# Softmax sums inverted on VectorE instead of ScalarE, VectorE operations over two PSUM banks, and new instruction orders in a three-part transformer block

## The chip, the cores and the metric

One core of one Trainium2 chip runs the whole program as one launch. The metric is the device time of an execution in microseconds (us); the time of a kernel is the median of its timed runs. The engines of the core that matter here are TensorE (PE in the rows; PEld is its loading of weights), VectorE (DVE), ScalarE (ACT), GpSimd (POOL) and SyncE (SP), which issues the DMAs.

## The reference

Input `x` is 4 x 1024 x 256 in float32. Three parts follow each other, each on a layer-normalised input and added to the residual:

```python
x = x + _L0_attn_ref(_layernorm(x), ...)              # 16 heads of 16: a gated delta rule with short convolutions
x = x + _L0_xattn_ref(_layernorm(x), ctx, ctx, ...)   # differential cross-attention on 64 context rows
x = x + _L0_ffn_ref(_layernorm(x), ...)               # depthwise conv, top 2 of 8 experts, a small GELU network

def _sdpa(q, k, v):                                    # in _L0_xattn_ref, 2 x 16 heads of 8
    scores = jnp.einsum('bhqd,bhkd->bhqk', q * SCALE, k)
    p = jax.nn.softmax(scores, axis=-1)
    return jnp.einsum('bhqk,bhkd->bhqd', p, v)
a1, a2 = _sdpa(q1, k1, v), _sdpa(q2, k2, v)
attn = a1 - lam * a2                                   # then a norm over 16 and a projection
```

The change touches the softmax of the cross-attention (its maxima, its sums) and, in the first part, small steps of the convolution and of the delta rule.

## The kernel before

The 1024 positions are worked in 8 blocks of 128, for all 4 batches at once (512 columns). Each block's work is cut into a `first` half (the delta rule) and a `second` half (cross-attention and the expert network). Work is pipelined over blocks: in pass i (the loop of `turns`, line 642) run the second half of block i-1, and three parts of the first halves of blocks i, i+1 and i+2. The passes run from -2 to 8. Passes -2 and -1 follow the order "start", pass 0 "head", passes 1 to 6 "steady", pass 7 "drain", pass 8 "last".

Inside a pass, nothing decides the order at run time: the table `ORDERS` lists for every engine and stage the names of its steps, one after the other. A step without a prefix belongs to the first half of block i, `+` to that of i+1, `*` to that of i+2, `-` to the second half of block i-1. Every engine works off its list in order, and waits at a step for semaphores that other engines raise (`up`, `fin`). An instruction that waits holds all that follow it on its engine. `KEEP` adds filler matmuls (line 1811) ahead of certain TensorE steps of the stages other than "steady".

The cross-attention of a block is worked in 8 units u, two per batch. Of a unit:

- `sc` (TensorE, line 2103): scores into two PSUM banks, half a = 0 and half a = 1, 512 columns (8 heads by 64 context rows) each. In the steady order these are banks 4 and 5, in the last pass banks 0 and 1 take turns with them.
- `max` (VectorE, lines 1582 and 1588): step 0 takes the maximum of each head, one reduction for each bank; step 1 subtracts it, one instruction for each bank. Each half's subtraction raises the semaphore `psub`, for which the next unit's scores into that bank wait.
- `max` (ScalarE, line 1037): the exponential of 1024 columns.
- `pt` (TensorE and ScalarE, lines 2125 and 1045): transposes in two halves, each copied out of PSUM.
- `pv` (TensorE, line 2139): the products with the values and with ones, so that the sums of the softmax stand in PSUM beside the numerators.
- `den` (ScalarE, lines 1053 and 1054): the reciprocal of the sums as exp(-ln(s)), 128x256: a logarithm out of PSUM into SBUF, then the exponential in place.
- `av` (VectorE, lines 1598 and 1601): numerator times reciprocal (semaphore `a_num`, for which the next unit's transposes into the same bank wait), and a1 - lam a2.

Steps of the first half that the change touches, all on VectorE: `conv` (lines 1353 and 1364 copy the three columns of halo in and out of `pre`, one block of 128 channels at a time, six each per pass), `dsel` and `gsub` (lines 1402, 1408, 1418: the decay matrix out of PSUM banks 2 and 3, one instruction for each bank), `zc` (line 1482: two instructions of 256 columns out of banks 2 and 3, eight times per pass). `solve` is a chain of small steps that inverts 16 x 16 triangles, `s`, `m` and `o` (lines 1499, 1492, 1510 and 1513) carry the state from chunk to chunk; they share VectorE with the attention in a pass.

The attention part of VectorE's steady order reads, in part:

```
-max.0.0 -max.0.1 -max.1.0 am.0 -max.1.1 am.1 -av.0.0 am.2 +cond -av.0.1 -max.2.0 -max.2.1 am.3 -av.1.0 solve.0.0
... -max.6.0 -max.6.1 zc.1 -av.4.1 -av.5.0 s.0 -max.7.0 zc.2 m.1 -max.7.1 -av.5.1 zc.3 -av.6.0
```

## Time and profile before

| what | value |
|---|---|
| median of 3 runs | 1374.06 us (1372.43 to 1379.7) |
| profiled execution | 1380.29 us, its span 1378.5 us |
| mean granted TensorE clock | 0.989 of full speed |
| busy, share of the span: TensorE / VectorE / ScalarE / GpSimd | 94% / 83% / 66% / 15% |
| instructions: TensorE / VectorE / ScalarE | 17045 / 3060 / 1760 |
| a pass of the steady order (mean of 6) | 155.4 us |

All times of rows are of the profiled execution and count from its span's start. Busy time is the union of an engine's instructions; an engine that waits for a semaphore is idle. On VectorE consecutive instructions overlap a little: the next begins before the one ahead of it has ended, so that durations add up to more than the time they hold the engine.

### The profile page before, as it was taken

The numbers are of one execution on the slowest core, as the hardware profiler recorded it, in microseconds if no ns is written. First come the engines' busy times: TensorE is split into PE (matmuls) and PEld (weight loads), VectorE is DVE, ScalarE is ACT, GpSimd is POOL, SyncE is SP. The second block draws the span as 40 slices with busy tenths as digits, with TensorE's granted clock in tenths as the row PEclk, the third lists the DMA queues.
The fourth block names the chain that finished last, engine by engine and source line by source line (L and its number), as shares of the span: only waits on it lengthen the run. The fifth ranks groups of instructions, "written<-read, shape, count | busy, mean of one in ns | idle before, by whom it ended". The sixth has DMA issues, their size and how long they took to land.

```text
span 1378.5 us, 40816 instructions
## 1 busy us (share of the span) xinstructions
PE 1291.2 (94%) x17045; PEld 838.7 (61%) x17077; DVE 1139.6 (83%) x3060; ACT 907.6 (66%) x1760; POOL 206.8 (15%) x204
## 2 busy tenths in 40 slices
PE   6988899899999999899999999999999989899998
PEld 5665666646765566646765566646765567646754
DVE  6567899988898989988898989988898878966763
ACT  2564477756877577756877577856877466644664
POOL 1031111102301122102301122102301112101000
PEclk9999999999999999999999999999999999999999
DMA  7021020101110020101100010101100001000000
GB/s 271 8 48 32 3 45 4 33 2 32 32 33 2 2 58 6 34 1 30 35 33 2 2 55 10 34 1 32 32 18 3 1 32 17 19 1 16 2 1 16
DMA packets 22782, 35.77 MB, mean 26 GB/s; under 512 B 1992, under 2 KB 18504, under 8 KB 22344
## 3 DMA queue, kind: packets, MB, share of 16 engines
q1 hardware_dynamic: 22600, 33.17, 8.6%
q8 instruction: 136, 2.23, 0.7%
q14 instruction: 46, 0.38, 0.1%
HBM read 20.56 MB, written 8.39 MB: 21 GB/s over the span
## 4 chain that ended last, share of the span: by engine, by line
PE 68%; DVE 16%; ACT 10%; issue 4%; DMA 1%; POOL 0%; SPq 0%; DVEq 0%; ACTq 0%
PE bank L2210 14%; PE four L1970 5%; PE bank L1884 5%; PE bank L1757 4%; PE bank L1782 4%; PE bank L2125 4%; PE bank L2103 3%; PE bank L2139 3%; PE four L1989 2%; PE four L1782 2%; PE bank L1886 2%; ACT L833 2%; PE bank L1811 2%; PE four L2014 2%; PE bank L1789 2%
## 5 line engine op out<-in xcount | busy, mean ns | idle before, releaser
L2210 PE MATMUL bank<-w_sb,cs 128*128 128x512 f32 x512 | 248.7, 602 | 2.9 <-ACT qkv L1109 0.4
L798 POOL TENSOR_TENSOR decayed<-state,pk 128x512 f32<-128x512 f32 x64 | 76.1, 1189 | 671.3 <-DVE state L1499 671.3
L2210 PEld LDWEIGHTS bank<-w_sb,cs 128*128 128x128 f32 x512 | 92.4, 189 | 95.8 <-issue 71.5
L1109 ACT ACTIVATE cs<-bank 128x512 f32<-128x512 f32 x112 | 66.9, 598 | 99.2 <-PE bank L1763 48.8
L833 ACT ACT_TABLE_LOAD x82 | 105.2, 1283 | 1.5
L1357 DVE SCALAR_TENSOR_TENSOR qkv<-pre,l_sb,qkv 128x512 f32<-128x512 f32 x144 | 101.6, 751 | 0.0
L1884 PE MATMUL bank<-hT,w_sb 128*128 128x512 f32 x192 | 95.2, 619 | 3.9 <-ACT hid L913 2.2
L1696 DVE SCALAR_TENSOR_TENSOR cs<-cs,rwt 128x256 f32<-128x256 f32 x196 | 88.2, 485 | 6.2 <-ACT cs L1109 2.8
L1045 ACT COPY cs<-bank 128x512 f32<-128x512 f32 x114 | 66.0, 579 | 41.3 <-PE bank L2125 41.2
L1582 DVE TENSOR_REDUCE pkc<-bank 128x8 f32<-128x512 f32 x116 | 74.3, 682 | 21.1 <-PE bank L2103 20.0
L1811 PEld LDWEIGHTS bank<-c_sb 128*128 128x128 f32 x588 | 74.6, 199 | 11.3 <-issue 10.3
L1811 PE MATMUL bank<-c_sb 128*128 128x128 f32 x588 | 81.1, 287 | 0.0
L1499 DVE SCALAR_TENSOR_TENSOR state<-four,c_sb,decayed 128x128 f32<-128x128 f32 x256 | 71.5, 341 | 9.5 <-PE four L2014 9.5
L1037 ACT ACTIVATE cs<-cs 128x1024 f32<-128x1024 f32 x60 | 63.2, 1053 | 24.2 <-DVE cs L1588 24.0
L2125 PE MATMUL bank<-c_sb,cs 128*128 128x128 f32 x456 | 72.6, 282 | 5.6 <-ACT cs L1045 2.4
L1970 PE MATMUL four<-kq,shared 64*64 64x48 f32 x2048 | 71.2, 224 | 5.5 <-POOL shared L780 4.6
L2014 PEld LDWEIGHTS four<-rq,shared 32*64 32x64 f32 x2048 | 45.7, 133 | 50.0 <-issue 31.9
L2014 PE MATMUL four<-rq,shared 32*64 32x64 f32 x2048 | 63.6, 231 | 13.4 <-issue 4.3
L1588 DVE TENSOR_TENSOR cs<-bank,pkc 128x512 f32<-128x512 f32 x116 | 74.2, 681 | 0.9
L1970 PEld LDWEIGHTS four<-kq,shared 64*64 64x64 f32 x2048 | 66.7, 140 | 13.3 <-issue 13.1
L1513 DVE SCALAR_TENSOR_TENSOR M<-four,c_sb,M 128x128 f32<-128x128 f32 x192 | 66.7, 347 | 4.0
L2020 PE MATMUL four<-shared,rq 32*64 32x64 f32 x2048 | 63.5, 232 | 4.8 <-issue 2.2
(297 smaller groups left out, 2990.9 us busy)
## 6 DMA issues: line engine op xcount, KB each, us to landing
xt<-in_x SPq DMA_DIRECT2D x8, 512.0 KB, 4.8
vscr<-qkv SPq DMA_DIRECT2D x8, 512.0 KB, 2.6
vT<-vscr SPq DMA_DIRECT2D x32, 128.0 KB, 4.5
Tm<-in_x SPq DMA_DIRECT2D x8, 512.0 KB, 3.8
out<-cs SPq DMA_DIRECT2D x8, 512.0 KB, 2.9
w_sb<-in_weights SPq DMA_DIRECT2D x1, 3680.0 KB, 19.1
rotb<-swapped SPq DMA_DIRECT2D x16, 128.0 KB, 2.3
swapped<-rota SPq DMA_DIRECT2D x16, 128.0 KB, 2.3
```

The source lines that it names most:

```text
L798: fin("dec", tt(decayed[:, :, :, :], state[:, :, :, :], eGC[:, c, :].unsqueeze(1).unsqueeze(3).to_broadcast([P, 4, G * B, DH]), ALU.mult))
L833: nc.scalar.preload_act_table_set(name)
L1357: ins = stt(dst, pre[:, n % 4, :, t:TB + t], L("conv", 4 * n + t, 4 * n + t + 1), dst, ALU.mult, ALU.add)
L1582: highest[a] = link(red(mx[:, a, :], sc[a], AX.X, ALU.max))
L1696: ins = stt(comb[:, b, :], src, wgt, comb[:, b, :], ALU.mult, ALU.add)
L1782: last = mm(dst[:, D * n:D * n + D], lhs[:, k, b * TB:b * TB + TB], rhs[:, k, :], start=False, stop=n == 1 and k == 1)
L1811: mm(bank[7 if i > 0 else 6][:, 0:P], ident, ident, start=True, stop=True)
L1884: mm(dst, ctrl[:, k, at:at + P], hT[:, k, :], start=k == 0, stop=False)
L1970: last = mm(bank[RAW[c % 4]][q, 48 * n:48 * n + 48], kqb[q, c % 2, n, :], kq[q, g, b, c, :, :].rearrange("p x t -> p (x t)"), start=True, ...
L2014: return mm(dst, zc_ring[p_, c % 4, 2 * a + g, 1, :], rq[p_, c % 2, (2 * a + g) * 64:(2 * a + g) * 64 + 64].rearrange("p (h v) -> p h v", ...
L2125: last = nc.tensor.transpose(turned_bank(j, u, n)[:, h * P:h * P + P], prob[:, 4 * n + h, :], ident)
L2210: mm(dst, x1T[:, k, b * TB:b * TB + TB], ew[:, k, ep * 512:ep * 512 + 512], start=k == 0, stop=False)
```

## The change

ScalarE's step `den` goes, with its two instructions per unit, and VectorE gets a step `den` with one reciprocal per unit, straight out of PSUM. Banks 4 and 5 become one tensor of two banks, as banks 0 to 3 are already, so that one VectorE instruction can span both. `max`, `dsel`, `gsub` and `zc` then take one instruction where they took two, and `conv` copies the halo of two channel blocks at once. For `zc` the constant `zx` is stored twice as wide. `psub` is raised once a unit instead of twice, so the scores of the next unit wait for the whole subtraction, and the first reduction waits for both halves of the scores. All five stages have new orders on all four engines, and `KEEP` has other counts.

```diff
         four = ctx.enter_context(nc.psum_tensor("four", [P, 4, 512], F32))
-        bank = [four[:, n, :] for n in range(4)] + [ctx.enter_context(nc.psum_tensor(f"bank{n}", [P, 512], F32)) for n in range(4, 8)]
+        four45 = ctx.enter_context(nc.psum_tensor("four45", [P, 2, 512], F32))
+        bank = [four[:, n, :] for n in range(4)] + [four45[:, n, :] for n in range(2)] + [ctx.enter_context(nc.psum_tensor(f"bank{n}", [P, 512], F32)) for n in range(6, 8)]
...
+        def both_scores(j, u):
+
+            return four[:, 0:2, :] if j == NI - 1 and (u % 2 or u >= 4) else four45[:, :, :]
...
-                def den_(u):
-                    log_exp()
-                    up("pv_ps", u + 1)
-                    if u:
-                        up("a_num", u)
-                    o_s = values_bank(j)[:, :].rearrange("p (f x t) -> p f x t", f=2, x=2)
-                    ch.do(A(den, o_s[:, :, 1, :], ACT.Ln))
-                    fin("den", A(den, den, ACT.Exp, scale=-1.0))
...
-                        for a, n in enumerate(pair):
-                            tap[a] = ch1.link(V.tensor_copy(pre[:, n % 4, :, 0:3], halo[:, n, :, :]))
+                        at = 2 * m % 4
+                        tap[0] = tap[1] = ch1.link(V.tensor_copy(pre[:, at:at + 2, :, 0:3], halo[:, 2 * m:2 * m + 2, :, :]))
...
-                        for a, n in enumerate(pair):
-                            fin("halo", V.tensor_copy(halo[:, n, :, :], pre[:, n % 4, :, TB:TB + 3]))
+                        at = 2 * m % 4
+                        fin("halo", V.tensor_copy(halo[:, 2 * m:2 * m + 2, :, :], pre[:, at:at + 2, :, TB:TB + 3]))
...
-                        for n in range(2):
-                            masked[n] = link(tt(M3[:, 32 * n:32 * n + 32, :], bank[2 + n][:, :].rearrange("p (n t) -> p n t", t=CH),
-                                                C("eye16").unsqueeze(1).to_broadcast([P, 32, CH]), ALU.mult))
+                        masked[0] = link(tt(M3[:, 0:NP_, :], four[:, 2:4, :].rearrange("p a (n t) -> p (a n) t", t=CH),
+                                            C("eye16").unsqueeze(1).to_broadcast([P, NP_, CH]), ALU.mult))
...
-                    zx = C("zx").unsqueeze(1).to_broadcast([P, G, P])
-                    for a in range(2):
-                        last = stt(zc_ring[:, c % 4, 2 * a:2 * a + 2, :, :].rearrange("p n x m -> p n (x m)"), bank[2 + a][:, 0:D].rearrange("p (n m) -> p n m", m=P), C("x0"), zx, ALU.mult, ALU.add)
-                    fin("zc", last)
+                    ring = flat(zc_ring[:, c % 4, :, :, :].rearrange("p n x m -> p n (x m)")).rearrange("p (a n) -> p a n", a=2)
+                    fin("zc", stt(ring, four[:, 2:4, 0:D], C("x0"), C("zx").unsqueeze(1).to_broadcast([P, 2, D]), ALU.mult, ALU.add))
...
                 def max_(u, k):
-                    sc = [scores(j, u, a)[:, :].rearrange("p (h n) -> p h n", h=8) for a in range(2)]
+                    sc = both_scores(j, u).rearrange("p a (h n) -> p (a h) n", h=8)
                     depth = 2 if j == NI - 1 else 1
-                    if k == 0 and j == NI - 1 and u:
-                        up("psub", 2 * u)
                     if k == 0:
-                        for a in range(2):
-                            up("sc_ps", 2 * u + a + 1)
-                            highest[a] = link(red(mx[:, a, :], sc[a], AX.X, ALU.max))
+                        if j == NI - 1 and u:
+                            up("psub", u)
+                        up("sc_ps", 2 * u + 2)
+                        highest[0] = link(red(flat(mx), sc, AX.X, ALU.max))
                         return
                     if u >= depth:
                         up("pt_ps", 2 * (u - depth) + 2)
-                    for a in range(2):
-                        ch.wait(highest[a])
-                        fin("psub", tt(prob_of(j, u)[:, 512 * a:512 * a + 512].rearrange("p (h n) -> p h n", h=8), sc[a], bc(mx[:, a, :], NK), ALU.subtract))
+                    ch.wait(highest[0])
+                    fin("psub", tt(prob_of(j, u).rearrange("p (h n) -> p h n", h=16), sc, bc(flat(mx), NK), ALU.subtract))
+
+                def den_(u):
+                    up("pv_ps", u + 1)
+                    o_s = values_bank(j)[:, :].rearrange("p (f x t) -> p f x t", f=2, x=2)
+                    fin("den", V.reciprocal(den, o_s[:, :, 1, :]))
...
-                    up("psub", 2 * (u - depth) + 1 + a) if u >= depth else up("qx_sb")
+                    up("psub", u - depth + 1) if u >= depth else up("qx_sb")
```

The same part of VectorE's steady order after the change:

```
-max.0.0 -max.0.1 am.0 -max.1.0 +cond -max.1.1 -den.0 -av.0.0 -av.0.1 am.1 am.2 -max.2.0 -max.2.1 am.3 -den.1 solve.0.0
... -max.6.0 -av.4.1 -max.6.1 zc.1 -den.5 -av.5.0 s.0 -max.7.0 zc.2 m.1 -max.7.1 -av.5.1 zc.3 -den.6
```

In the steady order `-max.u.1` stands right behind `-max.u.0` for u = 0 and u = 2. Summed over their entries, the fillers of `KEEP` are 119 in pass -1, 64 in pass 0, 63 in pass 7 and 44 in pass 8 before, and 109, 69, 54 and 44 after; pass -2 has 4 in both.

## Rows read from the trace of the kernel before

**Rows 1.** The page's first lines: busy us, share, instructions; then the chain's shares by engine.

```profile
PE 1291.2 (94%) x17045; PEld 838.7 (61%) x17077; DVE 1139.6 (83%) x3060; ACT 907.6 (66%) x1760; POOL 206.8 (15%) x204
...
PE 68%; DVE 16%; ACT 10%; issue 4%; DMA 1%; POOL 0%; SPq 0%; DVEq 0%; ACTq 0%
```

**Rows 2.** Stretches: length, busy us (instructions) of PE, PEld, DVE, ACT, POOL; granted clock, DMA, GB/s.

```profile
76.40:189.12 112.72, 97.18 (x1586) 67.71 (x1585) 89.55 (x234) 59.43 (x117) 22.41 (x22) 0.91 0.11 28
...
499.81:655.85 156.04, 148.97 (x2054) 94.28 (x2059) 138.82 (x372) 111.97 (x218) 25.31 (x24) 1.00 0.09 22
...
965.81:1121.55 155.74, 147.93 (x2038) 93.47 (x2043) 130.29 (x348) 107.35 (x212) 25.35 (x24) 0.98 0.06 16
1121.55:1269.40 147.85, 138.64 (x2073) 95.81 (x2079) 116.54 (x313) 86.96 (x178) 21.38 (x22) 1.00 0.05 13
1269.40:1378.50 109.10, 99.41 (x716) 65.43 (x717) 62.57 (x171) 61.03 (x113) 2.54 (x2) 1.00 0.03 11
```

**Rows 3.** Stretches of one steady pass, and the fullest 20 us of the neighbouring one.

```profile
499.81:579.81 80.00, 75.42 (x1262) 51.99 (x1266) 72.72 (x179) 63.39 (x132) 15.22 (x16) 1.00 0.12 29
579.81:655.85 76.04, 73.55 (x811) 42.30 (x797) 66.10 (x194) 48.58 (x87) 10.09 (x8) 1.00 0.06 15
...
404.93:424.93 20.00, 18.10 (x430) 11.41 (x416) 19.58 (x53) 17.15 (x37) 4.01 (x3) 1.00 0.02 4
```

**Rows 4.** VectorE's waits in one steady pass: who waited for whom, us, times, longest.

```profile
DVE cs L1598 <- ACT cs L1054: 2.6, 2, 1.8
DVE pkc L1582 <- PE bank L2103: 2.1, 1, 2.1
```

**Rows 5.** Groups by form: ScalarE's two steps, then VectorE's product: busy, mean ns, idle.

```profile
L1053 ACT ACTIVATE cs<-bank 128x256 f32<-128x256 f32 x56 | 21.0, 374 | 21.5 <-PE bank L2139 21.5
L1054 ACT ACTIVATE cs<-cs 128x256 f32<-128x256 f32 x64 | 26.7, 417 | 2.0
...
L1598 DVE TENSOR_TENSOR cs<-bank,cs 128x256 f32<-128x256 f32 x56 | 23.3, 417 | 16.7 <-ACT cs L1054 15.7
```

**Rows 6.** The chain through one unit: start us, us, what.

```profile
557.17 0.38 ACT cs L1053
...
558.02 0.44 DVE cs L1598
```

**Rows 7.** Reciprocals by form, a product of as few elements, then min/median/max of the reciprocals.

```profile
L1670 DVE RECIPROCAL rwt<-rwt 128x4 f32<-128x4 f32 x7 | 1.3, 180 | 0.2
...
L1671 DVE TENSOR_TENSOR rwt<-rwt 128x4 f32<-128x4 f32 x7 | 1.2, 167 | 0.2
...
L1670 DVE RECIPROCAL rwt<-rwt 128x2 f32<-128x2 f32 x2 | 0.3, 168 | 0.1
...
L1670 DVE RECIPROCAL rwt<-rwt x9: 167/180/183, 290.1 to 1338.2; 128x4 f32<-128x4 f32 x7, 128x2 f32<-128x2 f32 x2
```

**Rows 8.** VectorE's instructions in order of time, two places: start us, us, what.

```profile
509.09 1.22 DVE L1423 SCALAR_TENSOR_TENSOR M<-M,c_sb 128x1024 f32<-128x1024 f32 x1
510.23 1.29 DVE L1393 SCALAR_TENSOR_TENSOR kq<-kn,hid 128x512 f32<-128x512 f32 x2
...
538.71 1.28 DVE L1582 TENSOR_REDUCE pkc<-bank 128x8 f32<-128x512 f32 x2
539.91 1.28 DVE L1588 TENSOR_TENSOR cs<-bank,pkc 128x512 f32<-128x512 f32 x2
...
551.39 1.41 DVE L1357 SCALAR_TENSOR_TENSOR qkv<-pre,l_sb,qkv 128x512 f32<-128x512 f32 x2
552.72 0.87 DVE L1482 SCALAR_TENSOR_TENSOR shared<-four,c_sb 128x256 f32<-128x256 f32 x2
553.50 1.28 DVE L1582 TENSOR_REDUCE pkc<-bank 128x8 f32<-128x512 f32 x2
```

**Rows 9.** Stretches of passes 7 and 8 that hold the attention.

```profile
1121.55:1201.55 80.00, 74.74 (x1368) 58.40 (x1368) 71.70 (x178) 55.07 (x117) 14.62 (x17) 1.00 0.09 22
1280.00:1320.00 40.00, 38.76 (x449) 28.89 (x448) 30.02 (x64) 27.64 (x51) 0.00 (x0) 1.00 0.01 2
```

More of the change, by code:

```diff
@@ new lines @@
+        d1.0 -pw.1.0 -pw.0.1 -moe.6 wo.2 -pt.9 -pv.3 -turn5.1 -moe.5 -ffd.1 cs.4.1 *turn1.1 *rot -moe.9 cs.7.1 -moe.19
+        -sc.2.1 -sc.4.1 -turn4.1 d1.4 -moe.31 -wp.0.1 -pv.5 -sc.5.1 -moe.14 -pt.15 cs.6.1 cs.3.0 onorm.1 -pt.3 -moe.10
+        -pt.10 +sum.0 +sum.1 cs.4.0 -moe.29 -moe.25 cs.0.0 -qx.0.0 *gate.0 co.1 -sc.0.0 -moe.12 -pt.5 co.0 wo.1 z.3
+        -pt.4 -moe.16'''),
+        "dve": steps('''
+        solve.0.0 solve.11.0 am.1 -max.2.0 -acc.0.0 -dconv.1.0 zc.3 m.3 o.5.1 am.2 -av.6.1 -max.3.0 -max.0.0 +cond
@@ new lines @@
+        -sc.6.1 -pv.1 -moe.17 -ffu.1 cs.6.0 cs.6.1 -moe.18 -pv.0 -pv.5 -sc.7.0 *turn1.0 d1.7 -sc.5.1 *turn1.1 cs.7.0
+        -moe.21 -moe.31 cs.7.1 -moe.11 -moe.29 -moe.20 *rot co.0 -mo.0.0 -moe.0 co.1 -moe.3 onorm.0 -ffd.0 wo.0 -pt.11
+        -pv.3 onorm.1 -moe.25 -rturn.1 *gate.0 +sum.0 -pt.5 -qx.1.1 -ffd.1 -sc.7.1 wo.1 -mo.1.0 -pw.0.1 wo.2 +sum.1'''),
+        "dve": steps('''
+        -den.1 -av.7.1 norm.0 -av.6.1 -max.2.0 norm.1 dsel.0 -den.3 dsel.1 gsub.0 norm.2.0 -max.7.1 -hnorm.1 norm.3.0
@@ new lines @@
+        cs.7.0 cs.7.1 -turn6.1 *rot -router.0 co.0 co.1 -ffd.0 -ffd.1 onorm.0 -ffu.0 -ffu.1 onorm.1 *gate.0 wo.0
+        +sum.0 wo.1 wo.2 +sum.1'''),
+        "dve": steps('''
+        -ln2.0.0 norm.0 -ln2.1.0 -ln2.0.1 dsel.0 norm.1 -ln2.1.1 dsel.1 gsub.0 norm.2.0 norm.3.0 gsub.1 norm.2.1
+        norm.3.1 -max.0.0 -max.0.1 am.0 -max.1.0 +cond -max.1.1 -den.0 -av.0.0 -av.0.1 am.1 am.2 -max.2.0 -max.2.1
+        am.3 -den.1 solve.0.0 -av.1.0 solve.0.1 -av.1.1 solve.1.0 -max.3.0 solve.1.1 solve.2.0 +db solve.2.1 solve.3.0
@@ new lines @@
+        -moe.21 +proj.5.0 -turn5.0 cs.5.1 -moe.24 -moe.22 -moe.23 -moe.25 +sum.0 -moe.26 +proj.5.1 -moe.27 -moe.28
+        d1.6 -moe.30 -moe.29 -moe.31 -mo.0.0 cs.6.0 -mo.0.1 cs.6.1 *rot -turn5.1 -mi d1.7 -mo.1.0 -mo.1.1 cs.7.0
+        cs.7.1 *turn1.0 -turn6.0 -turn6.1 -ffd.0 co.0 co.1 -ffd.1 onorm.0 onorm.1 wo.0 +db -ffu.0 -ffu.1 wo.1 +gate.1
+        wo.2'''),
+        "dve": steps('''
+        norm.0 -ln2.0.0 -ln2.1.0 -ln2.0.1 dsel.0 dsel.1 -ln2.1.1 gsub.0 norm.1 gsub.1 norm.2.0 norm.3.0 norm.2.1
@@ new lines @@
+        -moe.23 -moe.24 -moe.25 -turn5.0 cs.1.1 co.1 +sum.0 -moe.26 +proj.5.1 z.2 cs.7.1 -moe.28 d1.7 +proj.2.0 cs.6.1
+        d1.2 cs.7.0 +proj.2.1 -moe.27 raw.2 -moe.29 cs.2.1 cs.4.1 raw.1 z.0 -moe.30 -moe.31 -mo.0.0 +proj.4.0 -turn5.1
+        -mo.0.1 -mi z.5 -mo.1.0 -mo.1.1 -turn6.0 -ffd.0 -turn6.1 -ffd.1 +proj.4.1 -ffu.0 sum.3 -ffu.1 cs.5.1 d1.1 wo.1'''),
+        "dve": steps('''
+        -ln2.0.0 o.4.3 -ln2.1.0 -ln2.0.1 solve.11.0 o.1.1 solve.13.0 s.5 -ln2.1.1 norm.2.1 +conv.0.0 solve.12.0
@@ L494, in scores @@
         def scores(j, u, a):
[L496 removed]
+            return both_scores(j, u)[:, a, :]
+        def both_scores(j, u):
+            return four[:, 0:2, :] if j == NI - 1 and (u % 2 or u >= 4) else four45[:, :, :]
         def score_depth(j, u):
@@ L1400, in decay @@
                         up("grow_ps")
-                        for n in range(2):
-                            masked[n] = link(tt(M3[:, 32 * n:32 * n + 32, :], bank[2 + n][:, :].rearrange("p (n t) -> p n t", t=CH),
-                                                C("eye16").unsqueeze(1).to_broadcast([P, 32, CH]), ALU.mult))
+                        masked[0] = link(tt(M3[:, 0:NP_, :], four[:, 2:4, :].rearrange("p a (n t) -> p (a n) t", t=CH),
+                                            C("eye16").unsqueeze(1).to_broadcast([P, NP_, CH]), ALU.mult))
                         return
                     link(V.tensor_copy(GCp.rearrange("p (g n) -> p g n", g=G), four[:, 2:4, CH - 1:512:CH]))
-                    for n in range(2):
-                        ch.wait(masked[n])
-                        link(red(Gp[:, 32 * n:32 * n + 32], M3[:, 32 * n:32 * n + 32, :], AX.X, ALU.add))
-                    masked[2] = ch.count
+                    ch.wait(masked[0])
+                    masked[2] = link(red(Gp, M3[:, 0:NP_, :], AX.X, ALU.add))
                     ch.wait(masked[2])
@@ L1416, in grow @@
                         ch.wait(masked[2])
-                        for n in range(2):
-                            last = tt(M2[:, 32 * n:32 * n + 32, :], bank[2 + n][:, :].rearrange("p (n t) -> p n t", t=CH),
-                                      bc(Gp[:, 32 * n:32 * n + 32], CH), ALU.subtract)
-                        masked[2] = link(last)
+                        masked[2] = link(tt(M2[:, :, :], four[:, 2:4, :].rearrange("p a (n t) -> p (a n) t", t=CH), bc(Gp, CH), ALU.subtract))
                         return
```

451 lines of the change are left out of this document (211 added, 240 removed).

## The prediction

> **What bounds the kernel now.** I read the page's engine shares and its chain first [rows 1]: TensorE is busy 94% of the span and holds 68% of the chain, VectorE 83% and 16%, ScalarE 66% and 10%. That average mixes stages, so next come stretches cut where a pass begins [rows 2]. Passes 1 to 6 of the steady order last 155.4 us each on average (189.12 to 1121.55, divided by six), pass 7 147.9, pass 8 109.1; what stands ahead of them, 189 us, has no attention in it. In a steady pass TensorE is busy 149.0 us and VectorE 138.8, or 89%: the first engine is nearly full, the second has 16.6 us to spare, the third, ScalarE (112 us), has 43. Cutting one pass in two [rows 3] shows where VectorE's room is: the first 80 us, which hold all eight attention units, use 72.7 us of VectorE, the rest 66.1 of 76.0. In the fullest 20 us of a neighbouring pass VectorE is busy 19.6. The waits on VectorE [rows 4] name ScalarE's reciprocal (line 1054) as the longest, 2.6 us a pass, twice in eight units; the next, 2.1 us, is a TensorE result. So the kernel is bound by TensorE with VectorE close behind, and this change takes work from the engine with the most room and gives it to the one with little.
>
> **What goes from ScalarE.** Per unit one logarithm of 374 ns and one exponential of 417 ns [rows 5], so 8 x 0.79 = 6.3 us a pass, of 112. Both use the table that the softmax's exponential beside them uses, and the orders of before and of the change give 82 table loads each, so no load goes. ScalarE isn't the bound, so the 6.3 us alone are worth nothing; worth something is the path from the values' sums to the numerator: in one unit on the chain the logarithm starts at 557.17 and VectorE's product at 558.02 [rows 6], 0.85 us, with whatever ScalarE still has queued in front.
>
> **What VectorE gets.** A reciprocal of 128x256 out of PSUM, which this trace doesn't hold. It holds reciprocals of 2 and 4 elements a partition, 168 and 180 ns [rows 7]: 6 ns for each further element; a product of two tensors of 4 elements takes 167. Carried to 256 elements: 168 + 254 x 6 = 1.69 us. Back to back an instruction of this engine gives way about 0.08 us before it ends (two reductions last 1.28 us and the next starts after 1.20 [rows 8]), so each holds the engine 1.61 us. Lower bound: the 13 ns by which 180 is over the product's 167 are a fixed cost and the stream is that of a product of 256 elements from PSUM, 417 ns [rows 5]: 0.43 us, held 0.35. Upper bound: from the fastest record of a reciprocal to the slowest, (183 - 167) / 2 = 8 ns an element [rows 7], 2.20 us, held 2.1. I take 1.61, since mean and slope of both sizes agree with it. That is 8 x 1.61 = 12.9 us a pass. The Trainium skill speaks against the change here: its page "VectorE: DVE Perf Modes", in the walkthrough of the 8-slice pipeline, says the reciprocal is a hardware iterative divide with a repeat count of eight. If each element took eight cycles of that page's 0.96 GHz, an estimate from the page is 2.13 us for the stream alone, and the time would be that of the rival "far slower" below. The rows' 6 ns are 5.8 such cycles, so the trace so far says the mild form of it.
>
> **What the merges give back.** Maxima and subtractions: two instructions of 512 hold 1.20 us, one of 1024 holds 1.14 (509.09 to 510.23) [rows 8], so 0.06 saved for each of 16 merges. But the subtraction now waits for the end of the one reduction (1.22 instead of 1.14) where it stands right behind it; in the new steady order that is so in two units of eight. 16 x 0.06 - 2 x 0.11 = 0.7 us. Next zc: two of 256 hold 0.78 us (552.72 to 553.50); one of 512 of the same operation holds 0.66 (two from 551.39 to 552.72) [rows 8]: 8 x 0.12 = 0.9. Halo copies: six in and six out become three and three; each of the six saved holds little more than the fixed part, 2 x 0.60 - 1.14 = 0.06 to 0.08 us, so 0.4 to 0.5. The decay's three pairs 3 x 0.06 = 0.2. Together 2.3 us a pass. Bounds: nothing, if waits eat it; by durations alone (16 x 0.14 for the maxima, from 2 x 0.68 against 1.22; 8 x 0.2 for zc; 6 x 0.17 for the copies, the time of a small instruction in [rows 7]; 3 x 0.14) 5.2. I take 2.3, because start times count the overlap. "VectorE: DVE Perf Modes" in the Trainium skill (section on the TRN2 errata) gives (N+151)/0.96 ns for a two-tensor operation, by which a merge saves 157 ns and the 16 save 2.5 us; the durations in the rows agree with that formula, the starts do not, and by it the pass would be 1.9 us shorter.
>
> **New waits.** The score matmuls of the next unit wait for the whole subtraction instead of its first half: up to 0.6 us on two banks. Behind that wait TensorE has other matmuls queued in order (transposes, projections of the next pass), and ScalarE's copies wait for those. The first maximum waits for both score halves, about 0.5 us later than now. Where VectorE is the later engine neither costs anything; elsewhere up to 1 us a unit, kept for the range. A reciprocal also keeps everything behind it on VectorE, solver, state and output steps, 1.61 us; in steady passes that is inside the sum, and TensorE's state products wait for it.
>
> **The sum.** VectorE per steady pass: 138.8 + 12.9 - 2.3 = 149.4 us, in 155.4: 96%. The first 80 us would carry 72.7 + 12.9 - 1.6 = 84.0. So some of its work moves behind, and what is late next is VectorE, not TensorE. How full can it run? Over 80 us it is now at 72.7/80 = 91%, over its best 20 us at 98% [rows 3]; the middle is 95%. 149.4/0.95 = 157.3, so 1.9 us a pass. Passes 1 to 5: +9.5. Pass 6, with 130.3 us of VectorE [rows 2]: its attention part is as full, its end isn't, +1.5. Pass 7: 71.7 of its first 80 us [rows 9] plus about 11.5 makes 83, and the stretch behind has room; +2. Pass 8 has the last block's attention alone: in 40 us VectorE is busy 30.0 [rows 9]; 12.9 - 0.7 more, of which the 10 idle us take some 6: +6. Start and head have only merges: -1. Fillers of TensorE (from the diff 119, 64, 63, 44 become 109, 69, 54, 44 in the four stages that have them) run where it waits; I cost them at nothing, and if that cover is gone it is 0.2 us each. Sum +18 on the profiled execution's 1380.3 us, whose span is 1378.5 with 1.8 around it: 1398. It lies 6 above the median of 1374.1; on that, **1392 us**.
>
> **Rivals.** *No change*: the fitted orders fill VectorE to 97%, giving 154.0 us, below the pass as it is, so TensorE still sets it; left are +6 in pass 8, +1 in pass 7, -1 ahead: 1380, less what a better order recovers of TensorE's 6.4 idle us a pass, say 0.7 in each: 1375. For it: all orders are new. It decides at 1.78 us held per reciprocal ((155.4 x 0.97 - 136.5) / 8). *Faster*: the reciprocal is near its lower bound, VectorE gains 0.5 us and loses the 2.6 us that it waits for ScalarE; -2 a pass over seven passes and -2 in pass 8 give 1358. The point is 0.61 us held, where 8 of them less 2.3 equal 2.6. Against it: 168 and 180 ns. A good fit of the orders alone would have to win over 1 us a pass for the same sign. *Far slower*: VectorE stays at 92% of the time, 162.4 us a pass, or the reciprocal holds 2.1 us: (136.5 + 16.8)/0.95 = 161.4. +6 to +7 in five passes, +4, +4, +8, -1: 1421. A TensorE that waits more may lose clock as well: in the head, at 86% busy, 0.91 was granted, in steady passes 1.00 [rows 2].
>
> **How the numbers follow.** Chances: forecast 0.50 (1380 to 1410), far slower 0.10 (up to 1428), no change 0.18, faster 0.22. Range 1360 to 1428: below lies part of the faster case, above the upper bound with a bad fit. About 0.5% (7 us) is what a measurement of this kernel can tell from no change; so faster than 1367: 0.22, within: 0.18, slower than 1381: 0.60.
>
> **What would show it.** A reciprocal row of 64 at about 1.7 us; VectorE near 149 us a steady pass and its share at 95%; no wait of the product for ScalarE; steady passes of about 157 us with TensorE's idle time up by 2; pass 8 longer by 6. Wrong, if the reciprocal lasts under 0.7 us, if a pass keeps 155 with VectorE at 97%, or if passes pass 160.

## The result and the profile after

The changed kernel takes 1462.11 us (median of 4 runs, 1452.76 to 1465.81) where the kernel before takes 1374.1: a ratio of 1.0623, 95% interval 1.0562 to 1.0684. It is slower by 88 us, not by the 18 that were forecast, and lies above the whole range.

The page of the changed kernel, its first line of busy times and its chain, to set beside [rows 1]:

```profile
PE 1304.2 (90%) x17049; PEld 843.7 (58%) x17049; DVE 1225.3 (84%) x2860; ACT 861.6 (59%) x1632; POOL 204.5 (14%) x204
...
PE 44%; DVE 38%; issue 8%; ACT 8%; DMA 1%; POOL 0%; SPq 0%; DVEq 0%; ACTq 0%
```

By shares little has happened: VectorE 83% before, 84% now, TensorE 94% and 90%. The chain tells more: VectorE's share went from 16% to 38%, TensorE's from 68% to 44%. An engine that is idle for 16% of the time has become the one that is waited for.

The stretches of [rows 2] in the changed kernel (length, busy us of PE, PEld, DVE, ACT, POOL, granted clock, DMA share, GB/s): head, a steady pass, pass 6, pass 7, pass 8.

```profile
74.96:180.97 106.01, 90.51 (x1592) 63.03 (x1591) 88.17 (x217) 59.10 (x117) 22.50 (x22) 0.98 0.12 29
512.48:677.21 164.73, 150.46 (x2058) 94.53 (x2059) 149.54 (x347) 106.14 (x202) 24.94 (x24) 0.99 0.08 21
1004.93:1171.49 166.56, 150.60 (x2042) 95.07 (x2043) 141.85 (x323) 101.41 (x196) 24.95 (x24) 0.96 0.06 14
1171.49:1334.50 163.01, 146.67 (x2060) 100.51 (x2061) 127.52 (x294) 81.56 (x162) 21.22 (x22) 0.95 0.06 14
1334.50:1450.70 116.20, 100.10 (x719) 65.88 (x717) 75.06 (x163) 56.02 (x97) 2.54 (x2) 0.99 0.02 6
```

The profiled spans differ by 1450.7 - 1378.5 = 72.2 us, less than the medians' 88: the profiled execution is the shortest of its kernel's four here, and before it is longer than all the timed ones. Passes 1 to 6 give 990.5 - 932.4 = +58.1, pass 7 +15.2, pass 8 +7.1, all ahead of pass 1 gives 181.0 - 189.1 = -8.1. VectorE's work in the steady pass is 149.5 us: the forecast had 149.4. So the price of the new work was right, and what was made of it was wrong.

Where in a pass the time lies shows when the pass is cut at the end of its last attention step (unit 7's a1 - lam a2) instead of at 80 us as in [rows 3]. The kernel before, pass 3:

```profile
499.81:572.88 73.07, 69.19 (x1179) 48.80 (x1179) 66.81 (x163) 58.26 (x123) 13.06 (x15) 1.00 0.13 31
572.88:655.85 82.97, 79.79 (x875) 45.48 (x880) 72.01 (x210) 53.71 (x95) 12.25 (x9) 1.00 0.05 14
```

The changed kernel, passes 2 and 4 cut the same way:

```profile
344.81:430.47 85.66, 73.97 (x1163) 51.52 (x1163) 78.31 (x147) 51.68 (x105) 13.48 (x15) 0.94 0.11 26
430.47:512.48 82.01, 79.52 (x900) 45.03 (x901) 71.52 (x201) 54.20 (x97) 11.46 (x9) 1.00 0.05 14
...
677.21:758.42 81.21, 69.43 (x1162) 48.81 (x1162) 77.73 (x147) 52.05 (x105) 13.49 (x15) 1.00 0.11 28
758.42:840.15 81.73, 79.40 (x900) 45.04 (x901) 71.62 (x202) 54.20 (x97) 11.46 (x9) 1.00 0.06 15
```

Over six passes the attention parts grow by 56.8 us, the parts behind them by 1.2. In the part behind TensorE is nearly full in both kernels (79.8 of 83.0 us before, 79.4 of 81.7 after). The attention part was 73.1 us with 66.8 of VectorE, and is 81.2 with 77.7. Pass 2 shows a second, smaller loss: with the same work TensorE is busy 74.0 us instead of 69.4, at a granted clock of 0.94. If all six passes lasted as long as pass 4 (162.9), the six would be 12.9 us shorter; these 12.9 go with granted clocks of 0.94 to 0.98 in the stretches concerned. Such a clock is a mean of TensorE's two levels: at 0.94 the engine ran at 1.2 instead of 2.4 GHz for 0.06 x 2 x 85.7 = 10 us of the stretch.

VectorE's waits in the attention part of pass 4 (who waited for whom: us in total, times, longest):

```profile
DVE rotb L1334 <- ACT rotb L826: 1.2, 1, 1.2
DVE M L1419 <- PE four L1956: 0.7, 1, 0.7
DVE pkc L1564 <- PE four L2089: 0.5, 1, 0.5
```

All three end within the first 19 us of the pass, ahead of the third unit's maxima. From there to the last unit VectorE is at no place idle for over 0.25 us. The waits of [rows 4] for ScalarE's inversion are gone, as forecast. The wait is TensorE's now: first the changed kernel in the same stretch, then the kernel before in the attention part of pass 3:

```profile
PE bank L2111 <- DVE cs L1584: 6.1, 4, 1.9
...
PE bank L2125 <- DVE cs L1598: 0.3, 1, 0.3
```

The transposes (line 2111, before 2125) wait for VectorE's product (line 1584, before 1598) to free their bank.

### The profile page after: what moved, and what is told of

Same layout as the page of the kernel before. It is cut to its first block, busy times and chain, and to the rows that moved or that the text cites. A ratio compares the mean times of both kernels' runs of the same rounds, so it can differ in the third digit from the quotient of the medians.

```text
span 1450.7 us, 40406 instructions
## 1 busy us (share of the span) xinstructions
PE 1304.2 (90%) x17049; PEld 843.7 (58%) x17049; DVE 1225.3 (84%) x2860; ACT 861.6 (59%) x1632; POOL 204.5 (14%) x204
## 4 chain that ended last, share of the span: by engine, by line
PE 44%; DVE 38%; issue 8%; ACT 8%; DMA 1%; POOL 0%; SPq 0%; DVEq 0%; ACTq 0%
PE four L2196 5%; PE bank L2196 4%; DVE cs L1569 4%; DVE cs L1574 4%; DVE pkc L1564 3%; PE bank L1870 3%; PE four L1768 3%; PE bank L1743 3%; DVE qkv L1348 3%; DVE cs L1682 2%; PE bank L1768 2%; DVE state L1482 2%; PE four L1775 2%; PE four L2089 1%; PE four L1920 1%
## 5 line engine op out<-in xcount | busy, mean ns | idle before, releaser
L798 POOL TENSOR_TENSOR decayed<-state,pk 128x512 f32<-128x512 f32 x64 | 70.8, 1107 | 756.8 <-DVE state L1482 756.8
L2196 PE MATMUL four<-w_sb,cs 128*128 128x512 f32 x284 | 139.4, 604 | 0.8 <-DVE cs L1628 0.2
L2196 PE MATMUL bank<-w_sb,cs 128*128 128x512 f32 x228 | 111.3, 605 | 2.6 <-ACT cs L1100 2.1
L1682 DVE SCALAR_TENSOR_TENSOR cs<-cs,rwt 128x256 f32<-128x256 f32 x196 | 97.4, 528 | 6.0 <-ACT cs L1100 1.8
L1574 DVE RECIPROCAL cs<-bank 128x256 f32<-128x256 f32 x56 | 97.9, 1748 | 3.2 <-PE bank L2125 3.0
L2111 PEld LDWEIGHTS bank<-c_sb,cs 128*128 128x128 f32 x456 | 53.2, 148 | 69.3 <-issue 67.5
L1564 DVE TENSOR_REDUCE pkc<-four 128x16 f32<-128x1024 f32 x64 | 77.9, 1218 | 11.3 <-PE four L2089 11.2
L2089 PE MATMUL four<-kbx,cs 32*128 32x256 f32 x512 | 77.0, 405 | 3.8 <-DVE cs L1569 1.9
L2196 PEld LDWEIGHTS four<-w_sb,cs 128*128 128x128 f32 x284 | 51.0, 190 | 47.2 <-issue 40.1
L1797 PEld LDWEIGHTS bank<-c_sb 128*128 128x128 f32 x560 | 71.2, 197 | 11.6 <-issue 10.8
L1569 DVE TENSOR_TENSOR cs<-four,pkc 128x1024 f32<-128x1024 f32 x60 | 73.2, 1220 | 5.3 <-PE bank L2111 3.8
L2000 PE MATMUL four<-rq,shared 32*64 32x64 f32 x2048 | 61.8, 230 | 16.7 <-DVE rq L1475 10.8
```

What stands on the lines that cost most here:

```text
L1564: highest[0] = link(red(flat(mx), sc, AX.X, ALU.max))
L1569: fin("psub", tt(prob_of(j, u).rearrange("p (h n) -> p h n", h=16), sc, bc(flat(mx), NK), ALU.subtract))
L1574: fin("den", V.reciprocal(den, o_s[:, :, 1, :]))
L1682: ins = stt(comb[:, b, :], src, wgt, comb[:, b, :], ALU.mult, ALU.add)
L1797: mm(bank[7 if i > 0 else 6][:, 0:P], ident, ident, start=True, stop=True)
L2000: return mm(dst, zc_ring[p_, c % 4, 2 * a + g, 1, :], rq[p_, c % 2, (2 * a + g) * 64:(2 * a + g) * 64 + 64].rearrange("p (h v) -> p h v", ...
```

## The theories

Theory A: the attention part is limited by VectorE alone, microsecond for microsecond, wherever in it the work falls, and VectorE's room behind the last unit is of no use to it. Rivals: B, VectorE's load over the whole pass counts, as the forecast assumed; C, it is not the reciprocal but the new orders or the merged operations; D, not VectorE's time counts but the delay between a unit's sums and its numerator.

The text uses the letters in this sense. Some expectations give B and C to rivals of their own, which their sentences name. Every ratio from here on is against the kernel before, run again with each group of experiments (medians 1373.1, 1373.1 and 1372.2 us). Edits are shown against the changed kernel, where nothing else is said, and cut at "...".

## The reciprocal's length against the pass

### A copy in its place

```diff
-                    fin("den", V.reciprocal(den, o_s[:, :, 1, :]))
+                    fin("den", V.tensor_copy(den, o_s[:, :, 1, :]))
```

> The changed kernel with a plain copy out of PSUM where the reciprocal stands, in every order and wait the same; the sums are not inverted, so that part of the computation is left out. Theory A (the attention part of a pass is VectorE's, and lasts as long as what VectorE has to do before unit 7 is through; room behind it can't be used): a copy holds VectorE about 0.34 us instead of 1.67, 8 x 1.33 = 10.6 us less ahead of unit 7, a steady pass falls from 165.1 to about 155 us, pass 8 by some 7, the whole from 1452 to 1375 (1362 to 1388). Rival B (the new orders fit badly, whatever the reciprocal takes) and rival C (the score matmuls that wait for a whole subtraction): at most 20 us less, over 1430.

Measured: 1368.67 us (1364.91 to 1372.41), ratio 0.9966 (0.9948 to 0.9984). With the same orders and merges, and the inversion cut to a copy of 0.42 us, the loss is gone. A hits. The expectation's own rivals, the new orders and the merged wait (both C of the list), are out by 60 us: C falls as the cause of the loss as a whole. B of the list isn't tested here, since the copy takes work out of the whole pass too. Pass 3, attention part and the part behind, then pass 7:

```profile
494.77:566.15 71.38, 69.08 (x1158) 48.67 (x1158) 67.51 (x147) 51.93 (x105) 13.52 (x15) 1.00 0.12 32
566.15:647.87 81.72, 79.42 (x900) 44.99 (x901) 71.60 (x201) 54.24 (x97) 11.47 (x9) 1.00 0.05 14
...
1106.60:1261.00 154.40, 144.40 (x2060) 98.97 (x2061) 117.31 (x294) 81.42 (x162) 21.20 (x22) 0.96 0.06 15
```

Pass 7 is the exception: with the copy it takes 154.4 us at a granted clock of 0.96, where the kernel before takes 147.9 at 1.00 [rows 2].

### Half a reciprocal

```diff
-                    fin("den", V.reciprocal(den, o_s[:, :, 1, :]))
+                    fin("den", V.reciprocal(den[:, :, 0:TB // 2], o_s[:, :, 1, 0:TB // 2]))
...
-                        fin("a_num", tt(ta, o_s[:, :, 0, :], den, ALU.mult))
+                        fin("a_num", tt(ta.rearrange("p f (a t) -> p f a t", a=2), o_s[:, :, 0, :].rearrange("p f (a t) -> p f a t", a=2),
+                                        den[:, :, 0:TB // 2].unsqueeze(2).to_broadcast([P, 2, 2, TB // 2]), ALU.mult))
```

> The changed kernel with the reciprocal over 64 of the 128 columns, used for both halves in the product (half of the sums are not inverted). Estimate: 168 + 126 x 6.2 = 0.95 us instead of 1.75, 0.80 less a unit, 6.4 us a pass. Theory A (dose for dose): eight passes with attention, 8 x 6.4 = 51 us less than 1462: 1411 us (1402 to 1422). Theory C (a threshold: up to some length the reciprocal hides in VectorE's room): within 6 us of the kernel with a copy, 1363 to 1375.

Measured: 1392.36 us (1389.84 to 1393.04), ratio 1.0134 (1.0110 to 1.0159). Less than A's range and more than that of the expectation's rival, a threshold: the step from the copy to half is 24 us, from half to the whole 70. The records of the reciprocal are 0.95 and 1.75 us. Pass 3:

```profile
498.07:573.12 75.05, 69.24 (x1163) 48.68 (x1163) 71.58 (x147) 51.93 (x105) 13.52 (x15) 1.00 0.11 30
573.12:654.87 81.75, 79.39 (x901) 44.95 (x901) 71.64 (x201) 54.25 (x97) 11.47 (x9) 1.00 0.05 14
```

In the stretches the dose is straight: attention 71.4, 75.05, 81.2 us for 67.5, 71.6, 77.7 us of VectorE, so 3.5 to 3.9 more than VectorE's work each time; behind it 81.7 in all three. The totals bend, and the granted clock, on which A had no say, bends with them: the runs with the copy have 0.985 to 0.994, those with half 0.990 to 0.992, those of the changed kernel 0.972 to 0.980. Among these last four, 1452.76 us goes with 0.980, 1459.56 with 0.975, 1464.65 and 1465.81 with 0.972. So of the 93 us between copy and change some 79 are the dose (8 passes by 162.9 - 153.1), if all eight lose alike; the other 15 are left for the clock. That is worked out, not shown: no run held the clock fixed.

## The same work in other places

The kernel with the copy gets eight more reciprocals of 100 columns in each steady pass; the edits are shown against it. Mean of one in the first of three kernels, 765 ns (769 in the other two):

```profile
L1579 DVE RECIPROCAL extra<-c_sb 128x100 f32<-128x100 f32 x48 | 36.7, 765 | 0.0
```

### Right behind each copy

```diff
+                def more(k):
+                    V.reciprocal(extra[:, :], c_sb[:, 0:100])
...
-        ... am.3 -den.1 solve.0.0 -av.1.0 ...
+        ... am.3 -den.1 -more.1 solve.0.0 -av.1.0 ...
```

> The changed kernel with the inversion cut to a copy (its output is not an inversion), plus eight extra reciprocals of 100 columns in every steady pass, one right behind each unit's copy, whose result nobody reads. Estimate from rows: 168 + 98 x 6 = 0.76 us each, 0.68 held, 5.4 us a pass, 33 us over six passes. Theory A (the attention part of a pass is VectorE's alone, so each microsecond that VectorE gets there lengthens the pass by the same): 1369 + 33 = 1402 us (1394 to 1412). Theory B (what counts is VectorE's load over the whole pass): the same time as the kernel in which these eight stand late in the pass, within 5 us.

Measured: 1395.42 us (1388.57 to 1396.17), ratio 1.0147 (1.0112 to 1.0181), 27 above the copy. A hits.

### Behind the last attention unit

```diff
-        ... -anorm.1 ... -top.1.0 ... -acc.3.0 ... -hnorm.0 ...
+        ... -more.0 -anorm.1 ... -more.1 -top.1.0 ... -more.2 -acc.3.0 ... -more.5 -hnorm.0 ...
```

> The same kernel with a copy for the inversion, and the same eight extra reciprocals of 100 columns a pass, but behind the last attention unit, between the expert and output steps. VectorE's work per pass is that of the kernel with the eight placed early. Theory A (behind the attention the pass is TensorE's, VectorE has room that it can use only there): 1369 to 1380 us. Theory B (load over the whole pass counts): as the kernel with the early eight, about 1400 us if each costs its time.

Measured: 1376.92 us (1370.42 to 1384.55), ratio 1.0023 (1.0003 to 1.0043), 8 above the copy and 18 below the early eight. A hits, B falls.

### Behind each unit's last step

```diff
-        ... -av.1.0 solve.0.1 -av.1.1 solve.1.0 ...
+        ... -av.1.0 solve.0.1 -av.1.1 -more.1 solve.1.0 ...
```

> The changed kernel with a copy for the inversion (its output is not an inversion) and eight extra reciprocals of 100 columns in every steady pass, as in the kernel that had them right behind each unit's copy, but here behind each unit's last step (a1 - lam a2), so that they stand between no sum and its numerator. Theory A (VectorE's time is what is short in the attention part, wherever in it the microsecond falls): the same as with the early eight, 1395 us (1388 to 1402). Theory D (the chain sums, inversion, product, next transposes is what sets the attention part, and VectorE has room beside it): 1369 to 1378, as the kernel with the copy alone or with the late eight.

Measured: 1390.88 us (1387.19 to 1394.45), ratio 1.0150 (1.0124 to 1.0177), 22 above the copy and in A's range. One of its eight stands behind unit 7 and so outside the attention part.

Pass 3 of the three, early (attention part), late (both parts), off the path to the numerator (attention part):

```profile
500.85:576.80 75.95, 69.22 (x1162) 48.69 (x1162) 72.54 (x155) 52.03 (x105) 13.49 (x15) 1.00 0.11 30
```

```profile
494.94:566.36 71.42, 69.09 (x1158) 48.68 (x1158) 67.56 (x147) 51.93 (x105) 13.50 (x15) 1.00 0.11 32
566.36:649.53 83.17, 79.50 (x900) 44.99 (x901) 75.99 (x209) 54.22 (x97) 11.30 (x9) 1.00 0.05 14
```

```profile
497.29:572.19 74.90, 69.44 (x1162) 48.75 (x1162) 71.42 (x154) 52.18 (x105) 13.52 (x15) 1.00 0.11 30
```

Equal work, two prices. In the attention part 5.0 us more of VectorE make it 4.6 longer, and 3.9 more in the third kernel 3.5 longer. Behind the last unit 4.4 us more of VectorE cost 1.5. So B falls, but the room there isn't quite free: about a third of what is put in comes out in the length.

The third kernel was to part A from D, and by itself it doesn't. Its extra reciprocals stand between no sum and its numerator in the list, but in time they do: a later unit's sums lie ready while VectorE still works on them. Unit 4 of pass 3, the last products with ones on TensorE and the numerator on VectorE (start us, us), first with the copy alone, then in the third kernel:

```profile
543.19 0.40 PE L2125 MATMUL bank<-cs,opair 128*32 128x128 f32 x8
545.43 0.39 DVE L1584 TENSOR_TENSOR cs<-bank,cs 128x256 f32<-128x256 f32 x1
```

```profile
546.93 0.40 PE L2130 MATMUL bank<-cs,opair 128*32 128x128 f32 x8
549.78 0.38 DVE L1589 TENSOR_TENSOR cs<-bank,cs 128x256 f32<-128x256 f32 x1
```

From the end of the one to the end of the other it is 2.2 us and then 2.8; over the eight units 12.7 us with the copy, 15.7 in the third kernel, 17.7 with the early eight. What speaks against D is VectorE's idle time. Length less work of the attention part is 3.9 us with the copy and 3.4 to 3.5 with half the reciprocal, with the early eight, in the third kernel and with the whole reciprocal. If the delay alone set the part, VectorE would idle more when the delay grows; it doesn't, so the length follows its work.

## The other parts of the change

### The merges alone, old orders

The edit in words, against the changed kernel:

```diff
-ORDERS, KEEP of the change
+ORDERS, KEEP of the kernel before; den stays ScalarE's logarithm and exponential
```

> The merged VectorE instructions alone, with the two banks as one tensor and the one wait a unit; the sums inverted on ScalarE, orders and fillers of before. Theory A: 1 to 2 us less of VectorE a pass, where it isn't alone at the bound: 1358 to 1374. Rival B: 1365 to 1380. Rival C: 0.6 us more in each of eight units, 5 us a pass, 1395 to 1420.

Measured: 1372.4 us (1369.76 to 1374.81), ratio 0.9998 (0.9983 to 1.0012). No difference to be measured. The time lies in the ranges of A and of the expectation's B, which overlap; its C, the merged wait, falls. Pass 3, attention part and the part behind, and VectorE's two longest waits in the first:

```profile
495.86:568.61 72.75, 69.29 (x1188) 48.91 (x1188) 65.33 (x138) 58.03 (x123) 13.03 (x15) 1.00 0.13 31
568.61:650.52 81.91, 79.83 (x880) 45.27 (x871) 71.35 (x201) 53.67 (x95) 11.58 (x9) 1.00 0.05 14
```

```profile
DVE cs L1581 <- ACT cs L1047: 3.0, 3, 1.8
DVE pkc L1566 <- PE four L2086: 2.4, 2, 2.1
```

In the attention part VectorE's work fell by 1.5 us (66.8 to 65.3) and the length by 0.3; the rest became waiting, 3.0 and 2.4 where [rows 4] has 2.6 and 2.1.

### The reciprocal alone, old orders

The edit against the kernel before:

```diff
-                    ch.do(A(den, o_s[:, :, 1, :], ACT.Ln))
-                    fin("den", A(den, den, ACT.Exp, scale=-1.0))
+                    fin("den", V.reciprocal(den, o_s[:, :, 1, :]))
...
-        ... -av.1.0 ...
+        ... -den.1 -av.1.0 ...
```

> The kernel before with the reciprocal on VectorE alone: its own orders, in which the reciprocal stands right ahead of the product, no merged instruction. Theory A: 12.9 us more for VectorE ahead of unit 7, less what it idled there (some 3), so passes of 165 to 168 us and 1455 to 1490 in all. Rival B: old orders, so only the forecast's 2 us a pass, 1385 to 1400. Rival C: no merged wait, so 1385 to 1410.

Measured: 1484.88 us (1480.82 to 1487.98), ratio 1.0818 (1.0780 to 1.0856). A hits.

### Reciprocal and merges, old orders

```diff
-        ... am.3 -den.1 solve.0.0 -av.1.0 ...
+        ... am.3 -den.1 -av.1.0 solve.0.0 ...
```

> The reciprocal on VectorE and the operations over two banks, with the orders and fillers of the kernel before (the reciprocal right ahead of its product). Compared with the kernel that has the reciprocal alone in the old orders (1484.9) it shows what the merges are worth when VectorE is short, compared with the changed kernel (1462.1) what the fitted orders are worth. Theory A: in the attention part the merges take 1.5 to 2.4 us from VectorE and now count in full, 6 x 1.5 to 6 x 2.4: 1468 to 1478 us; the orders give the rest. Theory C (merges are worth nothing, as in the kernel with merges alone; all of it is the orders): 1480 to 1490.

Measured: 1485.55 us (1479.7 to 1492.3), ratio 1.0846 (1.0806 to 1.0886). A misses: even where VectorE is short, the merges bring nothing in the old orders. Attention part of pass 3, the reciprocal alone and then with the merges:

```profile
523.33:608.83 85.50, 72.54 (x1190) 50.66 (x1190) 80.20 (x172) 53.35 (x107) 13.02 (x15) 0.98 0.11 27
```

```profile
523.71:608.97 85.26, 72.76 (x1190) 50.63 (x1190) 78.79 (x147) 53.36 (x107) 13.06 (x15) 0.98 0.11 27
```

1.4 us less work, 0.2 less time: 6.5 us of VectorE's idle time stay in this order, 3.5 in the fitted one. The fitted orders give back 85.3 - 81.2 = 4 us a pass, and 23 us in the medians (1485.55 to 1462.11); in both figures the granted clock is in it (0.98 against 1.00 in these stretches, 0.956 to 0.967 against 0.972 to 0.980 in the runs). With 66.8 us of work in 73.1 the kernel before wasn't limited by VectorE's time alone in this part; its order left VectorE idle for 6.3 us, 4.7 of them in the waits of [rows 4].

### The new orders, inversion back on ScalarE

```diff
-        "dve": ... -max.3.1 solve.3.1 -den.2 solve.4.0 ...
+        "dve": ... -max.3.1 solve.3.1 solve.4.0 ...
-        "act": ... +proj.0 -max.3 -pt.6 ...
+        "act": ... +proj.0 -max.3 -den.2 -pt.6 ...
```

> The changed kernel with the sums inverted on ScalarE again: its merged instructions, its orders on all engines and its fillers; ScalarE's step stands as soon as the order allows, behind the next unit's exponential and its own unit's second copy. Theory A: steady passes of 153 to 156 us, start and head 8 us shorter as in the changed kernel, 1350 to 1375. Rival B: passes stay over 160, over 1420. Rival C: 1400 to 1430.

Measured: 1405.82 us (1397.92 to 1408.83), ratio 1.0228 (1.0183 to 1.0274). A's number misses; the time lies in the range of the expectation's C, the orders and merges. A second kernel has ScalarE's inversion ahead of the exponential in the stages steady and drain, shown against the first:

```diff
-        "act": ... +proj.0 -max.3 -den.2 -pt.6 ...
+        "act": ... +proj.0 -den.2 -max.3 -pt.6 ...
```

> The changed kernel's orders and merged operations with the inversion back on ScalarE, as in the kernel that had it there behind the next unit's softmax exponential (1405.8), but in the stages steady and drain ahead of that exponential. There VectorE waited 5.2 us a pass for ScalarE's inversion. Theory A: VectorE has 65.6 us of work in an attention part of 74.9; without most of the waits the part takes 70 to 72, six passes gain 18 to 29 us and pass 7 some 3: 1375 to 1385. If the transposes and TensorE set it instead: 1400 to 1410.

Measured: 1397.64 us (1394.5 to 1398.56), ratio 1.0188 (1.0161 to 1.0214). That is 8 us below the first by the medians, with intervals that overlap, and in neither of the two ranges expected. Attention part and longest wait of VectorE, first kernel and then second:

```profile
496.46:571.30 74.84, 70.09 (x1170) 48.69 (x1177) 65.63 (x138) 56.77 (x120) 13.50 (x15) 1.00 0.12 30
```

```profile
DVE cs L1578 <- ACT cs L1044: 5.2, 6, 1.8
```

```profile
495.49:569.89 74.40, 70.05 (x1168) 48.64 (x1176) 65.89 (x138) 56.53 (x120) 13.51 (x15) 1.00 0.12 31
```

```profile
DVE cs L1578 <- ACT cs L1044: 3.5, 5, 1.0
```

VectorE's work here is as small as in the kernel with the merges alone, 65.6 to 65.9 us, and the part is longer. The wait fell by 1.7 us and the part by 0.4. The delay from sums to numerators fell too, from 16.4 to 12.8 us over the eight units, which D would have paid in full. So in this part the version is limited by its order, neither by VectorE's time nor by that delay.

Most of the loss lies elsewhere: passes 1 to 6 are 10.0 us longer than before, passes 7 and 8 together 23.9. The two passes in the first kernel, then before:

```profile
1124.22:1405.05 280.83, 251.24 (x2777) 167.76 (x2777) 176.81 (x441) 148.11 (x291) 23.73 (x24) 0.94 0.04 11
...
1121.55:1378.50 256.95, 238.05 (x2787) 161.24 (x2795) 179.12 (x484) 148.00 (x291) 23.92 (x24) 1.00 0.04 12
```

Orders fitted to an inversion on VectorE don't suit one on ScalarE. Whether a new fit for ScalarE's inversion would beat both kernels wasn't tried.

### Start and head alone

The edit in words, against the kernel before:

```diff
+ORDERS and KEEP of the change in the stages start and head, of the kernel before in the others; merges; den on ScalarE
```

> The kernel before with the operations over two banks, ScalarE's inversion kept, and the changed kernel's orders and fillers in the stages start and head alone. If the 8 us that the changed kernel is faster ahead of its first attention pass come from these orders: 1372.4 - 4 = 1368 us (1364 to 1370), the other half of the 8 us being granted clock. If it is the merges and the clock alone: 1372 (1370 to 1375).

Measured: 1374.25 us (median of 12 runs, 1369.81 to 1376.82 but for one of 5029.04, whose cause isn't known), ratio 1.0008 (0.9990 to 1.0026). The second alternative hits: the 8 us ahead of pass 1 are no gain of the change that a total would show. The head of this kernel, then that of the kernel with the copy, whose start and head are those of the change, then that of the kernel with the merges alone, in the old orders:

```profile
74.94:183.21 108.27, 92.57 (x1593) 63.42 (x1591) 88.15 (x217) 59.13 (x117) 22.57 (x22) 0.97 0.12 29
```

```profile
76.36:186.31 109.95, 93.96 (x1593) 64.40 (x1591) 90.81 (x217) 59.12 (x117) 22.42 (x22) 0.95 0.12 28
```

```profile
77.03:186.46 109.43, 95.19 (x1586) 65.72 (x1585) 88.23 (x217) 59.41 (x117) 22.41 (x22) 0.94 0.12 28
```

The new orders take 106.0 us at a granted clock of 0.98, 108.3 at 0.97, 110.0 at 0.95; the old ones 109.4 at 0.94, and 112.7 at 0.91 in the profiled execution before [rows 2]. At like clocks they don't differ.

### Work moved out of the attention part

```diff
-        ... -av.4.0 +conv.0.0 zc.0 ... -den.6 +conv.0.1 -av.6.0 ... -av.7.1 -ln3.0.1 +conv.0.2 ...
+        ... -av.4.0 zc.0 ... -den.6 -av.6.0 ... -av.7.1 -ln3.0.1 +conv.0.0 +conv.0.1 +conv.0.2 ...
```

> The changed kernel with two steps of VectorE's steady order, the halo copy with the first tap and the second tap of the first convolution pair (a copy of 0.3 us and four products of 0.75 us, 3.3 us), moved from the middle of the attention to behind its last unit. Theory A: the attention part gets 3.3 us shorter and the part behind has room: six passes, 20 us less than 1462: 1442 us (1434 to 1452). Theory B (load over the whole pass counts) or a TensorE that waits for the convolution: 1455 to 1475.

Measured: 1471.33 us (1466.04 to 1475.88), ratio 1.0715 (1.0675 to 1.0755). A misses here: by the medians 9 us more than the changed kernel, with intervals of the ratios that just touch, where 20 less were expected. Pass 3, then the attention part of pass 4:

```profile
520.85:602.76 81.91, 70.95 (x1162) 49.39 (x1163) 75.39 (x142) 51.71 (x105) 13.51 (x15) 0.98 0.11 28
602.76:687.34 84.58, 79.46 (x901) 44.98 (x901) 74.45 (x207) 54.25 (x97) 11.48 (x9) 1.00 0.05 14
687.34:768.61 81.27, 70.92 (x1162) 49.55 (x1162) 75.48 (x142) 51.75 (x105) 13.51 (x15) 0.98 0.11 28
```

VectorE's longest wait in the attention part of pass 3, with the clock just ahead of it, and its waits in that of pass 4 that the changed kernel doesn't have:

```profile
DVE cs L1569 <- PE bank L2111: 2.2, 1, 2.2
578.80:582.10 3.30, 3.30 (x8) 1.63 (x7) 2.05 (x3) 1.39 (x3) 0.00 (x0) 0.50 0.89 304
...
DVE cs L1569 <- PE bank L2111: 1.0, 2, 0.5
DVE shared L1466 <- PE four L1975: 0.7, 1, 0.7
DVE cs L1574 <- PE bank L2125: 0.6, 2, 0.5
```

VectorE's work in the part fell by 2.2 to 2.3 us and its length didn't. In pass 4 new waits for TensorE's results take 2.3 us in its place: subtractions wait for transposes, `zc` and reciprocals for matmuls. The convolution had filled such gaps. The clock has a part in it: in pass 3 TensorE ran at its lower level (0.50) from 578.8 to 582.1, and the wait for the transposes, from 580.85 on, is 2.2 us; in pass 4, where the clock fell earlier (718.8 to 722.1), the same wait is 0.5, but two others of 0.5 stand right behind the fall. Without these two some 1.3 us of new waits are left. Behind, 2.8 us more of work made 2.9 more of length, where the late reciprocals paid a third. The time is one that B had named too; B falls by the early and the late reciprocals, not here. So A's rule holds for work that is added to this order; taking work out pays only until the next wait is reached, here for more than half of it at once. No attention part of this run has a granted clock of 1.00, so that a gain of up to 1 us a pass may be hidden.

## Why the prediction was wrong, point by point

- **What bounds the kernel.** Right on the whole kernel, wrong in the pass: a pass is two stretches, one where VectorE's list must be through before the pass goes on and one where TensorE is nearly full. The cut of [rows 3] is 7 us too late to show them, though VectorE's share is 91% by either cut (72.7 of 80, 66.8 of 73.1).
- **ScalarE's 6.3 us.** Little, as forecast: the kernel with the copy has them gone too, with the merges and the new orders, and is 4 us faster than the kernel before. VectorE's wait of 2.6 us for them went, right.
- **The reciprocal.** Forecast 1.69 us from 2 and 4 elements, 1.61 held. The row:

```profile
L1574 DVE RECIPROCAL cs<-bank 128x256 f32<-128x256 f32 x56 | 97.9, 1748 | 3.2 <-PE bank L2125 3.0
```

  And VectorE's order of time in one unit, start us and us:

```profile
549.39 1.75 DVE L1574 RECIPROCAL cs<-bank 128x256 f32<-128x256 f32 x1
551.06 0.28 DVE L1452 TENSOR_TENSOR M<-Tm 128x176 f32<-128x176 f32 x1
```

  It holds the engine 1.67 us: right within 4%, 0.5 us a pass. The rivals' bounds of 0.43 and 2.20 us were both far off. In the kernel with half of it the row is

```profile
L1574 DVE RECIPROCAL cs<-bank 128x128 f32<-128x128 f32 x56 | 53.0, 946 | 1.0 <-PE bank L2125 0.9
```

  so it costs (1748 - 946) / 128 = 6.3 ns an element. By the Trainium skill, page "VectorE: DVE Perf Modes" (walkthrough of the 8-slice pipeline), the divide has a repeat count of eight; read as eight cycles an element at the page's 0.96 GHz that would be 2.13 us for the stream, an estimate from the page. The rows' 6.3 ns are 6.0 such cycles, so they don't bear that reading out.
- **The merges.** 2.3 us a pass of VectorE's time: right as work (138.8 to 136.7 in the kernel with the merges alone). As time worth nothing: with the old orders the kernels with and without them don't differ, whichever engine inverts. The new waits, kept for the range only, cost nothing there either.
- **The sum: the step that failed.** "So some of its work moves behind", and an average share of 95% over the pass. The sum itself had put 84.0 us of VectorE's work into the first 80. But nothing moved behind: VectorE's work behind the last unit is 71.6 us, 72.0 before and 71.4 with the merges alone, and its share of the pass is 91% (149.5 of 164.7). With the cut at the last unit the same terms give 66.8 + 8 x 1.67 - 1.5 = 78.7 us of work; with the 3.5 us that the changed kernel's trace shows idle there, 82.2 (measured 81.2), with the 6.3 of the kernel before, 85 (85.3 in the old orders). So the attention part, and with it the pass, grew by 8 us in the fitted orders and by 12 in the old, where the sum had 1.9. The second term that it put at nothing is the clock: 12.9 us over six passes go with it.
- **Passes 7 and 8.** Pass 8 +7.1 against +6: there the stretch was read by itself. Pass 7 +15.2 against +2: the same mistake, "the stretch behind has room", is 163.0 - 154.4 = 8.6 of it, if the kernel with the copy is taken as what the pass costs without the reciprocal. The other 6.5 are there with the copy too, at a granted clock of 0.96 (0.95 in the changed kernel, 1.00 before); how much of them is the new order of this pass and how much the clock stays open.
- **Start and head.** -8.1 against -1; 6.7 of it in the head, where the orders don't differ at like clocks, and no gain in the totals.
- **The rival "far slower"** named the right direction, a VectorE that stays at its share and a clock that falls. Its 162.4 us a pass are close to the 162.9 of pass 4, at a granted clock of 1.00, but by a share over the whole pass, which says nothing of the stretch where the time is lost: a near hit by luck. It priced the kernel at 1421 with 4 us each for passes 6 and 7 (measured 10.8 and 15.2) and no time for the clock. The sign to look for was there: wrong "if passes pass 160".
- **Fillers at nothing.** Those of start and head come with the kernel that takes over these two stages alone, which shows no loss; the others weren't tried apart. The price of 0.2 us for a filler has no row behind it.
